# Keeping the second attention's turned h for the shared expert, and one barrier instead of two between phases

## The chip, the cores and the metric

One core of a Trainium2 chip runs the whole program. The metric is device microseconds for one launch. The text uses these names for the engines: TensorE (PE in the rows, PEld for its weight loads), VectorE (DVE), ScalarE (ACT), GpSimd (POOL) and SyncE (SP), which issues most DMAs.

## The reference

Two layers, each of a cross-attention and a mixture of experts, on x of 16 batches x 128 tokens x 256 values:

```python
x = x + attention0(layernorm(x), ctx, ctx, bias, mask)          # 16 heads of 16
x = x + moe0(layernorm(x))                                       # top 2 of 14 experts, hidden 512
x = x + attention1(layernorm(x), ctx, ctx, causal or padding)    # 16 heads of 16
h = layernorm(x)
x = x + shared(h) + routed(h)    # shared expert, hidden 1024, and top 2 of 8 experts, hidden 1024
```

where `shared(h) = gelu(h @ Wfc_s + bfc_s) @ Wproj_s + bproj_s`, and the router's logits are `h @ Wr`. All in fp32.

## The kernel before

A tile is the 128 tokens of one batch (B = 16 tiles). The program is a row of six phases, written one after the other in `build`: `attention0`, `route_and_project` (routing of layer 0 and keys and values of the second attention), `experts` of layer 0 (45 slots of 128 rows), `attention1`, `shared_expert` (with the routing of layer 1), `experts` of layer 1 (39 slots). Each phase opens a block, in which every engine has its own hand-written list of instructions; semaphores alone order them across engines. What stands in the list is the order, nothing schedules it anew.

A block ends in a barrier of all engines. After it `end_phase` (L66 to L70) has GpSimd clear the semaphores of the phase (L68) and then sets a second barrier (L70), so that no engine begins the next phase before they are zero. I number the boundaries 1 to 5 by the phase that they end; a sixth ends the program.

`attention1` goes through the tiles in a loop in which a tile's stages are spread over several turns. For tile b, GpSimd's `layer_norm` (L1016) writes the normalized rows h into `Hn[:, b]`, SyncE's `store_h` (L960) writes them to memory for the later gather, five turns after the tile's own, TensorE's `turn_h` (L1155) transposes them into PSUM, ScalarE's `h_out` (L1309) copies that into the one buffer `hT`, and `logits` (L1194) multiplies `hT` by the router's weights. Tile 0 of the shared expert is done at the end of this phase, between the last attention tiles: `turn_shared` (L1161) transposes h of tile 0 a second time, VectorE copies it to `hx` (L1425), and `up_shared` (L1174) and `down_shared` (L1183) do the two products. Before that, `combine` (L1349) reads `Hn[:, b]` of layer 0.

`shared_expert` does the tiles 1 to 15 (N = 15). TensorE's list for turn n is: `up(n + 1)`, 16 fp32 matmuls in the program (the trace records each as 2); `turn(n + 2)`, the 2 transposes of h of a later tile (L1917); `down(n)`, 8 matmuls of 256 columns; and in turns 2 to 9 some products that invert the routing. ScalarE copies each turned tile from PSUM to `xT` (L1960) and applies the gelu (L1967). Only four PSUM banks take the results of `up`, so TensorE can do four of the eight hidden pieces before the first gelu. VectorE begins the phase with the top two of the logits; their difference (`diff`, L1610) goes through an exponential on ScalarE (L1973), which needs another table than the gelu, so that the gelu's table is loaded (L1974) after it. SyncE loads 16 MB of expert weights meanwhile, and stores the sums.

## Time and profile before

| | us |
|---|---|
| time before, median of 3 runs | 975.86 |
| lowest and highest of them | 975.44 and 976.85 |
| the profiled execution | 974.42 |
| its span, first to last instruction | 972.5 |
| TensorE busy | 922.1 (95% of the span) |
| VectorE, ScalarE, GpSimd busy | 511.5, 501.7, 436.8 |
| mean granted TensorE clock | 0.982 of 2.4 GHz |

The phases begin in the trace at about 0, 184.2, 221.8, 398.3, 554.2 and 676.2 us. The chain of work that ended last is, followed back, TensorE's from 678.7 us to 961.3 us, all of the last phase. A group of rows below gives one view of the trace. In a timeline a row has its start in us, its length, the engine, the line of the code, the operation with output and inputs, the count of merged instructions, and in square brackets the idle time before it and who ended it. A row of one line of the code has durations in ns (lowest, median, highest) and the starts of its first and last instruction in us.

### The profile page before, as it was taken

The numbers are of one execution on the slowest core, as the hardware profiler recorded it, in microseconds if no ns is written. First come the engines' busy times: TensorE is split into PE (matmuls) and PEld (weight loads), VectorE is DVE, ScalarE is ACT, GpSimd is POOL, SyncE is SP. The second block draws the span as 40 slices with busy tenths as digits, with TensorE's granted clock in tenths as the row PEclk, the third lists the DMA queues.
The fourth block names the chain that finished last, engine by engine and source line by source line (L and its number), as shares of the span: only waits on it lengthen the run. The fifth ranks groups of instructions, "written<-read, shape, count | busy, mean of one in ns | idle before, by whom it ended". The sixth has DMA issues, their size and how long they took to land. (4 is left out here: it accounts for less than half of the span.)

```text
span 972.5 us, 25476 instructions
## 1 busy us (share of the span) xinstructions
PE 922.1 (95%) x7420; PEld 830.1 (85%) x7421; DVE 511.5 (53%) x2152; ACT 501.7 (52%) x1425; POOL 436.8 (45%) x570
## 2 busy tenths in 40 slices
PE   5999999798999999789999899998999999999996
PEld 4788888697999999668878799997999999999996
DVE  3988988563444344279999553321333333333331
ACT  3877778233434343289999553332434334334332
POOL 5778885103555554535664420001244434434433
PEclk9999999899999999889999999999999999999999
DMA  8776674742222222353321299001111111111110
GB/s 263 236 229 202 185 240 149 286 137 93 70 70 70 71 69 65 127 168 88 91 62 44 69 376 341 18 28 33 34 59 53 51 56 46 47 53 54 50 33 1
DMA packets 98569, 107.36 MB, mean 110 GB/s; under 512 B 9858, under 2 KB 83992, under 8 KB 98234
## 3 DMA queue, kind: packets, MB, share of 16 engines
q1 hardware_dynamic: 88160, 80.76, 25.7%
q0 software_dynamic: 9936, 25.32, 8.7%
q8 instruction: 40, 0.66, 0.3%
q10 hardware_dynamic: 394, 0.31, 0.1%
q14 instruction: 39, 0.32, 0.1%
HBM read 86.68 MB, written 21.50 MB: 111 GB/s over the span
## 5 line engine op out<-in xcount | busy, mean ns | idle before, releaser
L2104 PEld LDWEIGHTS experts_bank<-xT,wp 128*128 128x128 f32 x1968 | 235.6, 194 | 8.4 <-issue 4.3
L2104 PE MATMUL experts_bank<-xT,wp 128*128 128x128 f32 x1968 | 236.3, 277 | 3.8 <-issue 2.0
L2146 ACT ACTIVATE Hn<-experts_bank,vecT 128x128 f32<-128x128 f32 x312 | 114.5, 367 | 167.5 <-PE experts_bank L2104 146.3
L1737 POOL DMA_INDIRECT rows<-token_rows,src x84 | 82.6, 984 | 179.9 <-DVE dst L1732 108.1
L2114 PE MATMUL experts_bank<-w,Hn 128*128 x624 | 142.6, 382 | 0.0
L2163 DVE COPY wp<-w 128x1024 f32 x123 | 90.4, 735 | 96.4 <-PE experts_bank L2104 95.5
L2114 PEld LDWEIGHTS experts_bank<-w,Hn 128*128 128x128 f32 x624 | 115.5, 190 | 15.8
L2146 ACT ACTIVATE hid<-experts_bank,vecT 128x128 f32<-128x128 f32 x180 | 66.0, 367 | 101.5 <-PE experts_bank L2104 92.0
L2114 PE MATMUL experts_bank<-w,hid 128*128 x360 | 85.0, 379 | 0.0
L2057 POOL DMA_INDIRECT out_dram<-yb,dst x39 | 41.2, 1056 | 90.2 <-DVE yb L2186 90.2
L1286 ACT ACTIVATE E<-U,mn 128x128 f32<-128x128 f32 x256 | 79.6, 392 | 2.2 <-DVE mn L1368 2.2
L648 ACT ACTIVATE w<-w,mn 128x128 f32<-128x128 f32 x256 | 80.0, 400 | 0.9 <-DVE mn L765 0.9
L2054 POOL DMA_INDIRECT token_outputs<-yb,dst x45 | 51.1, 1136 | 61.9 <-DVE yb L2177 61.9
L346 POOL TENSOR_TENSOR w<-w 128x1024 f32<-128x1024 f32 x32 | 75.6, 2365 | 0.9 <-DVE w L712 0.9
L1967 ACT ACTIVATE hid<-shared_bank,vecT 128x128 f32<-128x128 f32 x120 | 43.7, 367 | 60.5 <-PE shared_bank L1926 53.2
L2183 DVE TENSOR_TENSOR yb<-experts_bank,b 128x256 f32<-128x256 f32 x39 | 16.6, 425 | 110.5 <-PE experts_bank L2114 110.5
L2065 POOL DMA_INDIRECT X<-out_dram,dst x39 | 42.1, 1079 | 65.7 <-DMA out_dram<-yb,dst 62.6
L2114 PEld LDWEIGHTS experts_bank<-w,hid 128*128 128x128 f32 x360 | 65.0, 190 | 7.0
L1368 DVE CUSTOM_DVE_ANT_0 U<-attn_bank,M 128x128 f32<-128x128 f32 x256 | 57.8, 287 | 9.5 <-PE attn_bank L1101 9.3
L1926 PE MATMUL shared_bank<-xT,w_shared 128*128 128x128 f32 x480 | 57.9, 280 | 1.2 <-ACT hid L1967 1.2
L765 DVE CUSTOM_DVE_ANT_0 w<-attn_bank,w 128x128 f32<-128x128 f32 x256 | 57.4, 285 | 2.9 <-PE attn_bank L489 1.9
L1926 PEld LDWEIGHTS shared_bank<-xT,w_shared 128*128 128x128 f32 x480 | 56.5, 196 | 1.8 <-ACT hid L1967 1.5
(286 smaller groups left out, 1569.6 us busy)
## 6 DMA issues: line engine op xcount, KB each, us to landing
w<-in_fside_Bx16xSxS_dram SPq DMA_DIRECT2D x32, 512.0 KB, 4.9
w<-in_L_ffn_w_dram SPq DMA_DIRECT2D x28, 512.0 KB, 6.4
w<-in_L_ffn_Wfc_dram SPq DMA_DIRECT2D x8, 1024.0 KB, 13.8
w<-in_L_ffn_Wproj_dram SPq DMA_DIRECT2D x8, 1024.0 KB, 12.7
token_rows<-Hn SPq DMA_DIRECT2D x32, 128.0 KB, 4.6
y<-token_outputs SPq DMA_DIRECT2D x16, 256.0 KB, 3.2
ctx<-in_ctx_dram SPq DMA_DIRECT2D x26, 128.0 KB, 4.5
keys_values<-WT SPq DMA_DIRECT2D x12, 256.0 KB, 2.0
```

The costliest lines, as they stand in the source:

```text
L346: pool.tensor_tensor(fs[b % 2][:, heads], fs[b % 2][:, heads], bcast(amb[:, b:b + 1], [P, 8, P]), ALU.add).then_inc(bias_ready[half], 1)
L648: last = act.activation(E_[:, h], U[:, h], ACT.Exp, bias=mn[b % 2][:, h:h + 1], scale=-1.0)
L765: last = dve.tensor_tensor_reduce(U[:, h], scores_of(h), fs[b % 2][:, h], -twice, BIG, ALU.add, ALU.min, mn[b % 2][:, h:h + 1])
L1286: last = act.activation(E_[:, h], U[:, h], ACT.Exp, bias=mn[b % 2][:, h:h + 1], scale=-1.0)
L1368: last = dve.tensor_tensor_reduce(U[:, h], scores_of(h), c["M1"][:], -1.0, BIG, ALU.add, ALU.min, mn[b % 2][:, h:h + 1])
L1737: pool.indirect_dma_start(out=weights["rows"][:, n % 2], out_offset=None, in_=c["hn"], in_offset=bass.IndirectOffsetOnAxis(ap=routing["src ...
L1926: last = pe.matmul(HB[f % 4][:, 0:P], w1[:, i, f * P:(f + 1) * P], xT[n % 2][:, i], start=(i == 0), stop=(i == DC - 1))
L2054: pool.indirect_dma_start(out=c["yg"], out_offset=at_rows, in_=yb[n % 2][:], in_offset=None).then_inc(y_stored[n % 2], 16)
L2104: last = pe.matmul(HB[f % 4][:, 0:P], piece[:, i, (f % CF) * P:(f % CF + 1) * P], xT[par][:, i], start=(i == 0), stop=(i == DC - 1))
L2114: last = pe.matmul(Y[par][:, 0:D], hid[par][:, f], weights["w2"][:, bass.ds(e * (FC * D) + f * D, D)], start=(f == 0), stop=(f == FC - 1))
L2146: act.activation(hid[par][:, f], HB[f % 4][:, 0:P], moe.act, bias=bias).then_inc(hid_ready, 1)
L2163: dve.tensor_copy(wp[par if NP == 1 else q][:], of[:, :, q * PIECE:(q + 1) * PIECE]).then_inc(wp_ready, 1)
```

## The change

There are two parts.

**The barriers.** `end_phase` now only notes the semaphores of the phase as retired. The barrier at the end of each block stays; the second one is gone at boundaries 1 to 5. GpSimd clears the retired semaphores within the next phase: after its seven iotas in the two routing phases (L1842 and L1898 of the new file), after its four memsets in `attention1` (L1041), and after two gathers in `experts` (L2042). Semaphores of a phase and of the next are so never the same ones. At the program's end, clear and barrier stand as before.

**The turned h.** In `attention1` the normalized rows go into a ring of three buffers `hrow`, from which they are stored and transposed, and `h_out` copies the transposed tile from PSUM into `Hn[:, b]`, where it stays. The router's logits, tile 0 of the shared expert and `shared_expert` read it there. `turn_shared` with its copy, and all of `turn` and `in_out` of `shared_expert` go. `layer_norm` from tile 3 on waits until the tile three before has been transposed and its store has landed; the stores of layer 1 count on three semaphores, one for each buffer.

```diff
         def end_phase():
-            nc.clear_and_free_semaphores(phase_sems)
+            c["retired"] = list(phase_sems)
             phase_sems.clear()
-            nc.all_engine_barrier()
...
         experts(nc, sem, alloc, c, moe1, routing, weights, out)
-        end_phase()
+        nc.clear_and_free_semaphores(phase_sems)
+        nc.all_engine_barrier()
...
 def attention1
-        hT = sb("hT", [P, DC, P])
+        hrow = [sb(f"hrow{i}", [P, D]) for i in range(3)]
...
-        hx, hid = y[0][:, 0].rearrange("p (c t) -> p c t", c=DC), U[:, 0:FC]
+        hx, hid = c["Hn"][:, 0].rearrange("p (c t) -> p c t", c=DC), U[:, 0:FC]
...
             def store_h(b):
                 sp.wait_ge(h_ready, b + 1)
-                sp.dma_start(token_rows(c["hn"], b), c["Hn"][:, b]).then_inc(c["hn_stored"][1], 16)
+                sp.dma_start(token_rows(c["hn"], b), hrow[b % 3][:]).then_inc(c["hn_stored"][1][b % 3], 16)
...
-                pool.tensor_scalar(c["Hn"][:, b], c["X"][:, b], rs[:], nm[:], ALU.mult, ALU.add).then_inc(h_ready, 1)
+                if b >= 3:
+                    pool.wait_ge(hT_done, b - 2)
+                    pool.wait_ge(c["hn_stored"][1][b % 3], 16 * (b // 3))
+                pool.tensor_scalar(hrow[b % 3][:], c["X"][:, b], rs[:], nm[:], ALU.mult, ALU.add).then_inc(h_ready, 1)
...
+            nc.clear_and_free_semaphores(c["retired"])
             for b in range(-3, B + 1):
...
-            def turn_shared():
-                pe.wait_ge(h_ready, 1)
-                for i in range(DC):
-                    last = pe.transpose(IN[:, D + i * P:D + (i + 1) * P], c["Hn"][:, 0, i * P:(i + 1) * P], c["ident"][:])
-                last.then_inc(hx_done, 1)
...
             def h_out(b):
                 act.wait_ge(hT_done, b + 1)
-                if b >= 1:
-                    act.wait_ge(lg_done, b)
-                act.activation(hT[:].rearrange("p c t -> p (c t)"), IN[:, 0:D], ACT.Copy).then_inc(hT_ready, 1)
+                act.activation(c["Hn"][:, b], IN[:, 0:D], ACT.Copy).then_inc(hT_ready, 1)
...
-                if b == B - 1:
-                    dve.wait_ge(hx_done, 1)
-                    dve.tensor_copy(hx.rearrange("p c t -> p (c t)"), IN[:, D:2 * D]).then_inc(hx_ready, 1)
...
 def shared_expert
             route_counters(pool, r, iotas_ready)
+            nc.clear_and_free_semaphores(c["retired"])
...
             def up(n):
-                pe.wait_ge(xT_ready, n + 1)
...
-                        last = pe.matmul(HB[f % 4][:, 0:P], w1[:, i, f * P:(f + 1) * P], xT[n % 2][:, i],
+                        last = pe.matmul(HB[f % 4][:, 0:P], w1[:, i, f * P:(f + 1) * P], c["Hn"][:, S0 + n, i * P:(i + 1) * P],
...
-            turn(0)
-            turn(1)
             pe.wait_ge(shared["loaded"], 16 * 3)
             up(0)
...
-                if n + 2 < N:
-                    turn(n + 2)
                 down(n)
...
-            in_out(0)
-            in_out(1)
             act.wait_ge(diff_ready, 1)
...
                 tile(n)
-                if n + 1 < N:
-                    in_out(n + 1)
...
 def experts
             for n in range(2, AHEAD):
                 gather(n)
+            nc.clear_and_free_semaphores(c["retired"])
```

How the instructions stand now, at the two places on which the sum rests. A semaphore's name in brackets can be that of an earlier phase, whose number it got. First GpSimd at boundary 1, from the end of `attention0` to the first gather, before:

```order
L357 TENSOR_SCALAR Hn<-X,rs,nm 128x256 [waits nm_ready_117]
L145 UNCONDITIONAL_BRANCH
L68 ISA [waits barrier_Pool_Activation_PE_DVE_SP_gather]
L1846 UNCONDITIONAL_BRANCH [waits barrier_Pool_Activation_PE_DVE_SP_gather]
L1564 IOTA iota_e 128x14
...
L1572 IOTA pad_row 128x45
L1737 DMA rows<-token_rows,src 128x256 [waits hn_stored0,xn_ready_72]
```

and after:

```order
L358 TENSOR_SCALAR Hn<-X,rs,nm 128x256 [waits nm_ready_117]
L146 UNCONDITIONAL_BRANCH
L1839 UNCONDITIONAL_BRANCH [waits barrier_Pool_Activation_PE_DVE_SP_gather]
L1555 IOTA iota_e 128x14
...
L1563 IOTA pad_row 128x45
L1842 ISA
L1728 DMA rows<-token_rows,src 128x256 [waits hn_stored0_0,made_197]
```

The clear (the ISA row) has moved from between two barriers to behind the iotas, and one of the two waits for a barrier is gone. Second TensorE at the start of `shared_expert`, before:

```order
L1917 MATMUL shared_bank<-ident,Hn 128x128 x4
L1926 MATMUL shared_bank<-xT_348,w_shared 128x128 x16
L1926 MATMUL shared_bank<-xT_349,w_shared 128x128 x16
L1581 MATMUL shared_bank<-both,before 128x128
...
L1917 MATMUL shared_bank<-ident,Hn 128x128 x2
L1935 MATMUL shared_bank<-w_shared,hid_350 128x256 x8
L1926 MATMUL shared_bank<-xT_348,w_shared 128x128 x16
L1917 MATMUL shared_bank<-ident,Hn 128x128 x2
```

and after:

```order
L1911 MATMUL shared_bank<-Hn,w_shared 128x128 x32
L1572 MATMUL shared_bank<-both,before 128x128
L1573 MATMUL shared_bank<-both,ones 128x128
L1920 MATMUL shared_bank<-w_shared,hid_348 128x256 x8
L1911 MATMUL shared_bank<-Hn,w_shared 128x128 x16
```

The transposes (L1917) are gone, four at the start and two in front of each of the next thirteen `down`s, and nothing has come in their place.

## Rows read from the trace of the kernel before

**Rows 1.** Part 1 of the page: busy us, share of the span, instructions.

```profile
PE 922.1 (95%) x7420; PEld 830.1 (85%) x7421; DVE 511.5 (53%) x2152; ACT 501.7 (52%) x1425; POOL 436.8 (45%) x570
```

**Rows 2.** Busy time by stage, TensorE clock, DMA share, GB/s; columns are named first.

```profile
core 0: us, PE busy (x) PEld busy (x) DVE busy (x) ACT busy (x) POOL busy (x), PEclk, DMA share, GB/s
...
398.30:552.50 154.20, 147.05 (x1546) 119.80 (x1546) 124.47 (x705) 129.49 (x387) 77.09 (x180) 0.96 0.30 92
560.00:674.40 114.40, 114.31 (x798) 107.77 (x798) 35.93 (x158) 47.05 (x133) 8.37 (x12) 1.00 0.46 163
676.20:961.40 285.20, 283.30 (x1936) 265.71 (x1937) 105.12 (x191) 114.68 (x313) 116.36 (x112) 0.99 0.16 47
```

**Rows 3.** TensorE's queue at boundaries 1, 2, 4: first barrier, second barrier, and the clear.

```profile
L145 PEldq EVENT_SEMAPHORE  x2: 51/51/51, 182.2 to 183.1; - x2
...
L70 PEldq EVENT_SEMAPHORE  x1: 51/51/51, 184.1 to 184.1; - x1
...
L68 POOLq EVENT_SEMAPHORE_RANGE_CLEAR  x1: 527/527/527, 183.4 to 183.4; - x1
...
L1751 PEldq EVENT_SEMAPHORE  x2: 51/51/51, 219.9 to 221.2; - x2
...
L70 PEldq EVENT_SEMAPHORE  x1: 51/51/51, 221.7 to 221.7; - x1
...
L879 PEldq EVENT_SEMAPHORE  x2: 51/51/51, 552.6 to 553.3; - x2
...
L70 PEldq EVENT_SEMAPHORE  x1: 51/51/51, 554.2 to 554.2; - x1
```

**Rows 4.** Timeline at the start of the shared expert: start, us, engine, line, work [idle].

```profile
555.42 3.42 PE L1926 MATMUL shared_bank<-xT,w_shared 128*128 128x128 f32 x16
...
557.79 0.19 DVE L1610 TENSOR_TENSOR diff<-top 128x16 f32<-128x16 f32 x1
...
558.25 1.28 ACT L1974 ACT_TABLE_LOAD   x1
...
559.65 6.43 ACT L1967 ACTIVATE hid<-shared_bank,vecT 128x128 f32<-128x128 f32 x16
...
560.06 5.62 PE L1926 MATMUL shared_bank<-xT,w_shared 128*128 128x128 f32 x48 [1.21 <-ACT hid L1967]
```

**Rows 5.** Timeline of TensorE alone inside the shared expert, one turn and the last one.

```profile
569.64 3.73 PE L1926 MATMUL shared_bank<-xT,w_shared 128*128 128x128 f32 x32
573.21 0.38 PE L1917 MATMUL shared_bank<-ident,Hn 128*128 128x128 f32 x2
573.43 3.62 PE L1935 MATMUL shared_bank<-w_shared,hid 128*128 128x256 f32 x16
...
660.05 0.38 PE L1917 MATMUL shared_bank<-ident,Hn 128*128 128x128 f32 x2
```

**Rows 6.** Stretches around boundary 4, columns as in Rows 2.

```profile
552.20:555.60 3.40, 1.19 (x8) 0.66 (x7) 1.72 (x19) 0.38 (x1) 1.36 (x8) 1.00 0.11 8
555.60:559.05 3.45, 3.24 (x16) 2.95 (x15) 3.38 (x34) 2.68 (x4) 3.45 (x6) 0.51 0.89 337
```

**Rows 7.** Timeline where the second attention runs out of tiles.

```profile
537.11 0.42 DVE L1425 COPY y<-attn_bank 128x256 f32<-128x256 f32 x1
...
537.58 1.16 PE L1174 MATMUL attn_bank<-y,w_shared 128*128 128x128 f32 x8 [0.20 <-DVE y L1425]
```

**Rows 8.** Ring of h: store of h(0), making of h(3), landing times of the stores.

```profile
444.45 0.47 SPq L960 DMA_DIRECT2D token_rows<-Hn  x1
...
458.23 0.56 POOL L1016 TENSOR_SCALAR Hn<-X,rs,nm 128x256 f32<-128x256 f32 x1
...
DMA to landing us min/median/max: 1.7/2.7/4.3
```

More of the change, by code:

```diff
@@ L99, in build @@
         c["late_loaded"] = nc.alloc_semaphore("late_loaded")
-        c["hn_stored"] = [nc.alloc_semaphore(f"hn_stored{layer}") for layer in range(2)]
+        c["hn_stored"] = [[nc.alloc_semaphore(f"hn_stored{layer}_{i}") for i in range(n)] for layer, n in ((0, 1), (1, 3))]
         moe0 = Moe(0, 14, 512, a["L0_ffn_w1"], a["L0_ffn_w2"], a["L0_ffn_b2"], ACT.Gelu)
@@ L258, in store_h @@
                 sp.wait_ge(h_ready, b + 1)
-                sp.dma_start(token_rows(c["hn"], b), c["Hn"][:, b]).then_inc(c["hn_stored"][0], 16)
+                sp.dma_start(token_rows(c["hn"], b), c["Hn"][:, b]).then_inc(c["hn_stored"][0][0], 16)
             load_fs(0, 0)
@@ L929, in attention1 @@
         s_done = sem("s_done")
-        hx_done, hx_ready, up_done, hid_ready, down_done = (
-            sem("hx_done"), sem("hx_ready"), sem("up_done"), sem("hid_ready"), sem("down_done"))
+        up_done, hid_ready, down_done = sem("up_done"), sem("hid_ready"), sem("down_done")
         late_turned, late_T_ready = sem("late_turned"), sem("late_T_ready")
@@ L1154, in turn_h @@
                 for i in range(DC):
-                    last = pe.transpose(IN[:, i * P:(i + 1) * P], c["Hn"][:, b, i * P:(i + 1) * P], c["ident"][:])
+                    last = pe.transpose(IN[:, i * P:(i + 1) * P], hrow[b % 3][:, i * P:(i + 1) * P], c["ident"][:])
                 last.then_inc(hT_done, 1)
-            def turn_shared():
-                pe.wait_ge(h_ready, 1)
-                for i in range(DC):
-                    last = pe.transpose(IN[:, D + i * P:D + (i + 1) * P], c["Hn"][:, 0, i * P:(i + 1) * P], c["ident"][:])
-                last.then_inc(hx_done, 1)
             def up_shared(first, end):
                 if first == 0:
-                    pe.wait_ge(hx_ready, 1)
+                    pe.wait_ge(hT_ready, 1)
                     pe.wait_ge(shared["loaded"], 16 * 3)
@@ L1193, in logits @@
                 for i in range(DC):
-                    last = pe.matmul(Y[:, 0:E], hT[:, i], wr[:, i], start=(i == 0), stop=(i == DC - 1))
+                    last = pe.matmul(Y[:, 0:E], c["Hn"][:, b, i * P:(i + 1) * P], wr[:, i], start=(i == 0), stop=(i == DC - 1))
                 last.then_inc(lg_done, 1)
@@ L1244, in _ @@
                     turn_e(b, 1)
-                if b == B - 1:
-                    turn_shared()
                 if has(b - 1):
@@ L1422, in _ @@
                     minima(b, 3)
-                if b == B - 1:
-                    dve.wait_ge(hx_done, 1)
-                    dve.tensor_copy(hx.rearrange("p c t -> p (c t)"), IN[:, D:2 * D]).then_inc(hx_ready, 1)
                 if has(b + 3):
@@ L1743, in gather_first @@
     pool.wait_ge(made, 4)
-    pool.wait_ge(c["hn_stored"][moe.layer], 16 * B)
+    stored = c["hn_stored"][moe.layer]
+    for i, sem in enumerate(stored):
+        pool.wait_ge(sem, 16 * ((B + len(stored) - 1 - i) // len(stored)))
     for n in range(2):
@@ L1868, in shared_expert @@
         two = range(2)
-        xT = [sb(f"xT{i}", [P, DC, P]) for i in two]
         hid = [sb(f"hid{i}", [P, FC, P]) for i in two]
@@ L1877, in shared_expert @@
                         for k in (r["hot"][0], r["hot"][1], r["tmp"], r["over"])]
-        bank = [stack.enter_context(nc.psum_tensor(f"shared_bank{i}", [P, 512], F32)) for i in range(8)]
-        T, R, HB, Y = bank[0], bank[1], bank[2:6], bank[6:8]
+        bank = [stack.enter_context(nc.psum_tensor(f"shared_bank{i}", [P, 512], F32)) for i in range(7)]
+        R, HB, Y = bank[0], bank[1:5], bank[5:7]
         slots_of = R[:, 2 * B * moe.E:2 * B * moe.E + 2 * S]
@@ L1884, in shared_expert @@
         bias_added = sem("bias_added")
-        xT_done, xT_ready = sem("xT_done"), sem("xT_ready")
         hid_done, hid_ready = sem("hid_done"), sem("hid_ready")
@@ L1912, in _ @@
         def _(pe):
-            def turn(n):
-                if n >= 1:
-                    pe.wait_ge(xT_ready, n)
-                for i in range(DC):
-                    last = pe.transpose(T[:, i * P:(i + 1) * P], c["Hn"][:, S0 + n, i * P:(i + 1) * P], c["ident"][:])
-                last.then_inc(xT_done, 1)
             def up(n):
-                pe.wait_ge(xT_ready, n + 1)
                 for f in range(FC):
@@ L2070, in _ @@
                 gather(n)
+            nc.clear_and_free_semaphores(c["retired"])
             if out is not None:
```

5 lines of the change are left out of this document (removed).

## The prediction

> **What bounds the kernel now.** I read the page's busy times first: TensorE is busy for 95% of the span, no other engine for more than 53% [rows 1]. An average over phases says little, so the second view is the busy time by stage [rows 2]. From 560.0 to 674.4 us, the shared expert, TensorE is busy for 114.31 of 114.40 us, while ScalarE has 47 us of work and VectorE 36. From 676.2 to 961.4 us it is 283.3 of 285.2. In the second attention TensorE has 147 of 154 us, with ScalarE at 129 and VectorE at 124: nearly bound, with less room beside it. So anything taken from TensorE's list in the shared expert should be seen whole, work taken from ScalarE or VectorE there should not be seen, and time in which all engines stand still is on the path whatever bounds the phases. That is what the third view looks for: TensorE's own semaphore instructions at the boundaries [rows 3].
>
> **The second barrier.** At boundary 1 TensorE leaves the first barrier at 183.1 us and the second at 184.1 us, and between them stands GpSimd's clear of 0.53 us: 1.0 us. At boundary 2 it is 221.2 to 221.7, 0.5 us; at boundary 4 it is 553.3 to 554.2, 0.9 us [rows 3]. Boundaries 3 and 5 read like 2, 0.5 us each, so there are three of that kind. The sum is 1.0 + 3 x 0.5 + 0.9 = 3.4 us. No engine does anything in these stretches, and each next phase starts with a chain that begins at its barrier, so I count them whole. The bounds are 0, if what follows waits for something older than the barrier, and 3.4.
>
> The clears do not vanish. They stand in GpSimd's list behind the iotas, the memsets or two gathers. What is queued behind them is the bias additions of the shared expert, the clipping of the first tile in the attention, and the third gather and first fetch of sums in the experts. A clear with its drain is at most about 0.7 us by the one at boundary 1 (0.53 us, [rows 3]). GpSimd has 8.4 us of work in 114 us of the shared expert and half of the time free in the attention [rows 2], so I count nothing; if the first tile's chain of the attention had no room, it would be 0.7 us once.
>
> **The transposes of the shared expert.** TensorE starts the transposes of a turn at 573.21 us and the next product at 573.43 us: 0.22 us from start to start, though a transpose is drawn as longer, since they overlap. There are thirteen such pairs, the last at 660.05 [rows 5], all in the stretch in which TensorE is full. 13 x 0.22 = 2.9 us, bounds 2.7 and 3.0 for the rounding of the starts. The fifteen copies of ScalarE there lie beside TensorE's work and give nothing.
>
> The first two transposes of the phase are another matter. They stand ahead of the first sixteen recorded matmuls, which run from 555.42 to 558.84, but then TensorE waits 1.21 us for ScalarE's gelu [rows 4]. The gelu starts at 559.65, directly behind the load of its table (558.25, 1.28 us), that waits for the exponential, and that for VectorE's difference at 557.79 [rows 4]. VectorE begins at the barrier and its list does not change. So the early start of TensorE only makes the wait longer: gain 0 for the transposes, beyond the 0.9 us already counted. VectorE's list is the next late thing, and it was before.
>
> **The second transpose of tile 0.** At the end of the attention two transposes and a copy go. VectorE's copy runs from 537.11 to 537.53 us and TensorE's product starts at 537.58, after 0.20 us of idle time [rows 7]. Without them TensorE could start 0.22 + 0.20 = 0.4 us earlier. ScalarE's exponentials of tile 15 do not come earlier by that, so TensorE meets them again soon after. I take 0.2 us, bounds 0 and 0.4.
>
> **The ring.** GpSimd makes h(3) at 458.23 us; in the changed kernel that waits for the store of h(0), which SyncE issues at 444.45 us. The stores land within 4.3 us at the longest, so it is there by 448.8, 9.4 us early [rows 8]. Every tile has the same distance, since store and h both move on by one tile per turn. The transposition of the tile three before stands in TensorE's list ahead of the product that h needs. Cost 0. ScalarE loses a wait for the logits that had long been met, VectorE reads the same buffer as before: 0.
>
> **The clock.** Here the change can lose something. In the stretch from 552.2 to 555.6 us TensorE is busy for 1.19 of 3.40 us, and in the one behind it, to 559.05 us, the granted clock is 0.51, that is the 1.2 GHz level [rows 6]. The sixteen matmuls that fell into it took 3.42 us [rows 4]; at 2.4 GHz thirty-two take 3.57 us from start to start [rows 5], so sixteen take 1.8. These 1.6 us cost nothing before, since TensorE waited for the gelu anyway. In the changed kernel the sixteen matmuls start right behind the barrier at full clock, are through about 1.9 us later, and then TensorE stands still until the gelu. The gelu's first result lets it go on at 560.06, 5.9 us after the barrier's 554.2, so the pause grows from 1.2 to about 4 us. A slow stretch after that pause falls on matmuls that bound the phase. The bounds are 0 and 1.6 us; I take 1.1, since part of the slow stretch may still lie in the pause.
>
> The Trainium skill (TensorE: Matmul & The Clock Gate, Part 1) says that throttled is the default state and that activity releases it, and Part 4 that transposes do not count as activity. The rows agree with the first: the clock fell behind a thin stretch. By the page a pause of 4 us costs the clock nearly always, which would put the term at its upper bound.
>
> **Sum.** 3.4 + 2.9 + 0.2 - 1.1 = 5.4 us. Against the profiled execution that is 974.42 - 5.4 = 969.0. That execution lies 1.4 us below the median of the three runs, 975.86, and the change will be measured against a median: 975.86 - 5.4 = 970.5 us.
>
> **The rivals.**
>
> (a) *The slow clock costs more.* Besides the pause at boundary 4, a second slow stretch may move from hidden onto bound work, at another boundary, for the phases now meet the clock's ups and downs at other moments. For it speaks that boundary 4's slow stretch was wholly hidden; against it that each other pause gets shorter. Price: 1.6 instead of 1.1 and 1.6 more, 975.86 - 6.5 + 3.2 = 972.6. [...]
>
> (b) *The barriers give nothing.* If a phase's start were held by something else, such as the fetch of its code or a DMA issued long before, only the transposes pay: 975.86 - 2.9 - 0.2 + 1.1 = 973.9. Against it: TensorE starts each phase within about 0.1 us of the second barrier's release, at 184.2 behind 184.1.
>
> (c) *The clock comes back.* With shorter pauses one boundary no longer loses the clock, and the pause at boundary 4 costs nothing: 975.86 - 6.5 - 1.6 = 967.8. Against it: the pauses shrink only by 0.5 to 1.0 us.
>
> (d) *Slower: the ring holds the attention.* GpSimd would stand in `layer_norm`, and `v_in` and `normed` of the next tiles are queued behind it, for which TensorE waits. It decides from the point at which a store lands more than 458.23 - 444.45 = 13.8 us after its issue. Thirteen tiles wait so; at 1 us each the time is 975.86 - 5.4 + 13 = 983.5. Against it stand 4.3 us as the longest landing [rows 8].
>
> **How the numbers follow.** A run of this kernel can be told from no change at about 0.2%, 2.0 us. Chances: forecast 0.68, own range 968.8 to 972.0 (terms at their bounds: 3.4 + 3.0 + 0.4 = 6.8 at best, 3.4 + 2.7 + 0 - 1.6 = 4.5 at worst, and some tenths for the scatter of 1.4 us of the runs); (a) 0.07; (b) 0.12, half of it within 0.2%; (c) 0.08; (d) 0.05. Faster: 0.68 + 0.07 + 0.06 + 0.08 = 0.89; same 0.06; slower 0.05. The range of 8 in 10 takes in the forecast and (a), and the near side of (b) and (c): 968.0 to 973.2.
>
> **What would show it.** In the changed profile: no second stop behind a block's barrier, and first work of the next phase 0.1 us after it; the product of `down` directly behind that of `up` in the shared expert, 0.22 us earlier in each turn; TensorE idle for some 4 us at the start of the shared expert with the gelu still 5.4 us behind the barrier; a clock below 1.00 right behind that pause; the tiles of the attention at an unchanged distance, and no idle time of GpSimd in front of `hrow`. A longer distance of the tiles, or a phase whose first row is later than its barrier by half a microsecond, would prove me wrong.

## The result: faster by 9 us, more than forecast, and the profile after

| us | before | changed |
|---|---|---|
| median | 976.36 of 4 runs (975.44 to 976.91) | 967.16 of 4 runs (967.05 to 967.47) |
| the profiled execution | 974.42 | 967.47 |
| its span | 972.5 | 965.3 |
| TensorE busy | 922.1 | 917.9 |
| mean granted TensorE clock | 0.982 | 0.983 |

The ratio is 0.9905, 95% interval 0.9886 to 0.9923: 9.2 us less, where 5.4 were forecast, and 967.2 lies below the range of 968.0 to 973.2. Between the two profiled executions the gain is 6.95 us. The kernel before scatters more than the first three runs showed: 77 runs of it, taken beside the experiments, lie between 972.8 and 979.8 us, 28 of them above 977, with a median of 976.0. Ten runs of the changed kernel lie between 965.7 and 968.0. So the profiled execution of the kernel before, 974.4, is one of its shorter ones, and 2.3 of the 9.2 us can't be found by comparing these two profiles.

Part 1 of the changed kernel's page, which answers to [rows 1]:

```profile
PE 917.9 (95%) x7388; PEld 826.6 (86%) x7389; DVE 511.5 (53%) x2151; ACT 496.9 (51%) x1410; POOL 436.7 (45%) x570
```

TensorE has 32 recorded instructions and 4.2 us less, ScalarE 15 and 4.8 us less. TensorE's queue at the boundaries 1, 2 and 4 in the changed kernel (instruction, count, ns, start of first and last), and GpSimd's clear behind boundary 1, answer to [rows 3]:

```profile
L146 PEldq EVENT_SEMAPHORE  x2: 51/51/51, 182.4 to 183.3; - x2
...
L1744 PEldq EVENT_SEMAPHORE  x2: 51/51/51, 220.1 to 221.4; - x2
...
L880 PEldq EVENT_SEMAPHORE  x2: 51/51/51, 549.6 to 550.2; - x2
...
L1842 POOLq EVENT_SEMAPHORE_RANGE_CLEAR  x1: 526/526/526, 184.6 to 184.6; - x1
```

There is one stop where there were two, and the phases begin 0.1 us behind it: 183.4, 221.5, 550.3. The clear of boundary 1 lies 1.3 us into the next phase.

What the stops cost is best read as TensorE's idle time in front of the first matmul of phases 2 to 6. It was 2.12, 2.02, 4.53, 1.73 and 1.86 us and is 1.10, 1.50, 3.71, 0.84 and 1.34 us, 3.8 us less in all. At boundary 3 it is 0.8 us less, where the forecast has 0.5. The second release stood 0.54 us behind the first there, as forecast; the other 0.3 us are GpSimd's part of the first barrier, which took 0.38 us before and takes 0.1 us now. The rows of boundary 3, before and changed:

```profile
398.33 0.82 PE L1054 MATMUL attn_bank<-ident,WT 128*128 128x128 f32 x4 [4.53 <-PEq L70]
```

```profile
395.50 0.63 PE L1058 MATMUL attn_bank<-ident,WT 128*128 128x128 f32 x4 [3.71 <-PEq L1980]
```

The start of the shared expert in the changed kernel, all engines, as a timeline; it answers to [rows 4]:

```profile
550.33 1.19 DVE L1596 MAX8 top<-LG 128x8 f32<-128x8 f32 x16 [0.38 <-PEq L880]
550.33 2.02 PE L1911 MATMUL shared_bank<-Hn,w_shared 128*128 128x128 f32 x16 [0.84 <-PEq L880]
...
553.85 0.40 DVE L1601 TENSOR_TENSOR diff<-top 128x16 f32<-128x16 f32 x1
...
554.51 1.28 ACT L1947 ACT_TABLE_LOAD   x1
...
555.92 1.60 ACT L1942 ACTIVATE hid<-shared_bank,vecT 128x128 f32<-128x128 f32 x5
556.32 6.28 PEld L1911 LDWEIGHTS shared_bank<-Hn,w_shared 128*128 128x128 f32 x41 [4.16 <-ACT hid L1942]
556.32 6.36 PE L1911 MATMUL shared_bank<-Hn,w_shared 128*128 128x128 f32 x40 [3.97 <-ACT hid L1942]
```

The first sixteen matmuls now take 2.02 us instead of 3.42, then TensorE stands still for 3.97 us until the gelu at 555.92, which is 5.7 us behind the barrier (5.4 before). The stretches of that start, with busy time of each engine, granted clock (the column after POOL), DMA share and GB/s, answer to [rows 6]:

```profile
550.30:552.40 2.10, 2.02 (x16) 1.86 (x16) 2.04 (x29) 1.27 (x1) 1.21 (x8) 1.00 0.40 78
552.40:556.30 3.90, 0.00 (x0) 0.00 (x0) 3.83 (x25) 1.99 (x5) 3.90 (x7) 1.00 1.03 382
556.80:560.20 3.40, 3.40 (x19) 3.40 (x18) 1.63 (x6) 1.71 (x5) 3.40 (x6) 0.50 1.05 389
```

Behind the pause the clock is at its lower level of 1.2 GHz for 3.4 us, and TensorE is busy in all of it: 19 matmuls there, where a full-clock stretch of this length has 32 (below). Before, the slow stretch lay ahead of a wait.

TensorE alone inside the shared expert, as in [rows 5], and the ring as in [rows 8] (making of h, stores, landings), changed kernel:

```profile
563.86 3.62 PE L1920 MATMUL shared_bank<-w_shared,hid 128*128 128x256 f32 x16
567.31 3.73 PE L1911 MATMUL shared_bank<-Hn,w_shared 128*128 128x128 f32 x32
570.88 1.46 PE L1920 MATMUL shared_bank<-w_shared,hid 128*128 128x256 f32 x6
...
L1019 POOL TENSOR_SCALAR hrow<-X,rs,nm x16: 554/555/556, 432.6 to 546.2; 128x256 f32<-128x256 f32 x16
...
L960 SPq DMA_DIRECT2D token_rows<-hrow x16: 319/432/466, 442.0 to 546.8; - x16
...
DMA to landing us min/median/max: 1.7/2.8/4.2
```

The product of `down` stands directly behind that of `up`: from 567.31 to 570.88 are 3.57 us, and in [rows 5] it was 3.57 + 0.22. The tiles of the attention are (546.2 - 432.6) / 15 = 7.57 us apart. In the kernel before they were 7.62 us apart. The difference stands in three places. Between the tiles 13 and 14, where the second transpose of tile 0 is gone, the distance is 7.22 instead of 7.50 us, and so in every kernel with the turned h. Between the tiles 7 and 8 and between 10 and 11 it is 7.8 instead of 7.9 and 8.05 us, 0.4 us in all, and so in every kernel with one barrier per boundary, `barriers_only` among them, and in no other; why is open.

To see where the 7.2 us of the two spans went, I cut both at the first matmul of each phase. The time of a boundary counts to the phase that it ends. All times are us.

| phase with its boundary | before | changed | gain | forecast |
|---|---|---|---|---|
| 1 `attention0` | 184.2 | 183.4 | 0.9 | 1.0 |
| 2 `route_and_project` | 37.6 | 38.1 | -0.5 | 0.5 |
| 3 `experts`, layer 0 | 176.5 | 174.0 | 2.4 | 0.5 |
| 4 `attention1` | 155.9 | 154.8 | 1.1 | 1.1 |
| 5 `shared_expert` | 122.0 | 120.4 | 1.5 | 2.3 |
| 6 `experts`, layer 1, to the end | 296.3 | 294.5 | 1.8 | 0 |

Phases 2 and 3 differ from the forecast mostly by the clock. At the start of phase 3 the stretch of the kernel before and the same one of the changed kernel read (columns as above):

```profile
224.00:228.80 4.80, 4.35 (x24) 4.38 (x25) 1.55 (x3) 1.47 (x4) 1.18 (x1) 0.64 0.35 99
...
223.90:228.00 4.10, 3.94 (x35) 3.97 (x36) 1.40 (x3) 2.46 (x7) 0.89 (x1) 1.00 0.36 107
```

In exchange the slow stretch around boundary 1 is longer in the changed kernel, 10.2 us instead of 6.8. Further profiles of both kernels show that this comes and goes from execution to execution (below). Phase 6 is another matter. The end of the kernel before and of the changed one, as timelines:

```profile
964.93 0.43 DVE L2183 TENSOR_TENSOR yb<-experts_bank,b 128x256 f32<-128x256 f32 x1 [2.51 <-PE experts_bank L2114]
966.53 1.02 POOL L2065 DMA_INDIRECT X<-out_dram,dst  x1 [2.80 <-issue]
968.76 0.48 DVE L2186 SCALAR_TENSOR_TENSOR yb<-yb,share,X 128x256 f32<-128x256 f32 x1 [3.41 <-DMA X<-out_dram,dst]
```

```profile
959.11 0.42 DVE L2155 TENSOR_TENSOR yb<-experts_bank,b 128x256 f32<-128x256 f32 x1 [2.51 <-PE experts_bank L2086]
959.27 1.02 POOL L2036 DMA_INDIRECT X<-out_dram,dst  x1 [1.35 <-DMA out_dram<-yb,dst]
961.50 0.49 DVE L2158 SCALAR_TENSOR_TENSOR yb<-yb,share,X 128x256 f32<-128x256 f32 x1 [1.97 <-DMA X<-out_dram,dst]
```

The last fetch of sums starts 1.60 us behind VectorE's bias addition before, and 0.16 us after. Before, nothing recorded ends GpSimd's idle time ahead of it ("issue"). That is 1.44 us which no step of the prediction has, and it repeats: the time from the end of TensorE's last drain to the end of the span is 7.72 or 7.73 us in all six profiles of the kernels whose only clears stand between the barriers, and 6.3 to 6.7 us in all nine with clears inside the phases (6.27 or 6.28 in the six of the changed kernel and its variants, 6.58 in `spare_clear`).

### The profile page after: what moved, and what is told of

It reads as the page before. It is cut to its first block and busy times, and to the rows that moved or that the text cites. A ratio compares the mean times of both kernels' runs of the same rounds, so it can differ in the third digit from the quotient of the medians.

```text
span 965.3 us, 25316 instructions
## 1 busy us (share of the span) xinstructions
PE 917.9 (95%) x7388; PEld 826.6 (86%) x7389; DVE 511.5 (53%) x2151; ACT 496.9 (51%) x1410; POOL 436.7 (45%) x570
## 5 line engine op out<-in xcount | busy, mean ns | idle before, releaser
L1911 PE MATMUL shared_bank<-Hn,w_shared 128*128 128x128 f32 x480 | 58.2, 281 | 4.8 <-ACT hid L1942 4.0
L1911 PEld LDWEIGHTS shared_bank<-Hn,w_shared 128*128 128x128 f32 x480 | 56.8, 197 | 5.6 <-ACT hid L1942 4.2
```

Of the source, the lines that this page charges most:

```text
L1911: last = pe.matmul(HB[f % 4][:, 0:P], w1[:, i, f * P:(f + 1) * P], c["Hn"][:, S0 + n, i * P:(i + 1) * P], start=(i == 0), stop=(i == DC - 1))
```

## The experiments

Each ratio is against the runs of the kernel before on the same chip. Because of the scatter the time of the profiled execution stands beside the median.

**The two parts apart, and both kernels again.** `barriers_only` takes all edits of `end_phase` and the clears, and nothing of the turned h; `turned_only` the rest. `base_again` and `after_again` are the two kernels.

```diff
 barriers_only
         def end_phase():
-            nc.clear_and_free_semaphores(phase_sems)
+            c["retired"] = list(phase_sems)
             phase_sems.clear()
-            nc.all_engine_barrier()
...
 turned_only
         def end_phase():
             nc.clear_and_free_semaphores(phase_sems)
             phase_sems.clear()
             nc.all_engine_barrier()
...
-            turn(0)
-            turn(1)
             pe.wait_ge(shared["loaded"], 16 * 3)
```

> The kernel before, unchanged, timed again beside itself. Theory A (the profiled execution of before, 974.42 us, was a lucky one; the clock and the last fetch of sums scatter by some us from execution to execution): times between 974.4 and 977, median about 976.3, and in this profile more of TensorE's matmuls at 1.2 GHz, or the fetch of the last sums again more than 1 us after the landing that it waits for. Theory B (nothing scatters, the first profile shows what every execution does): the profile again at 974.4 and the same slow stretches.

> Only the barriers are changed, h is turned twice as before. Theory A (a second barrier costs the distance between the two releases, 3.4 us in all, and up to one slow stretch of the clock of 1.6 us comes or goes): 971 to 973 us against 976.4. Theory B (a barrier costs more than that distance, since the phase behind it starts warmer or its DMAs earlier): 969 to 970.5, 6 us or more off.

> Only the turned h is kept, both barriers stand as before. Theory A (13 pairs of transposes at 0.22 us and 0.2 us at the end of the attention, less a slow stretch of 1.6 us behind the longer pause at the start of the shared expert): 1.5 to 3.1 us off, 973.3 to 974.9 against 976.4. Theory B (the stores or copies of the attention matter too): more than 4 us off, and a shorter distance of the attention's tiles than 7.78 us.

> The changed kernel, unchanged, timed again. 967.2 us as before by both theories. Theory A: the slow stretches of the clock lie at other moments in this profile than in the first, in number between five and seven, and their place decides within 1 us. Theory B: they lie at the same places.

| kernel | median us (range, runs) | ratio, 95% | profiled execution | phases 1 to 6 of it |
|---|---|---|---|---|
| before, beside these | 975.74 (973.05 to 979.79, 23) | | | |
| `base_again` | 978.08 (973.7 to 979.72, 12) | 1.0023 (1.0009 to 1.0038) | 973.7 | 183.5, 37.4, 176.4, 155.9, 122.0, 296.6 |
| `barriers_only` | 969.2 (968.25 to 973.81, 6) | 0.9949 (0.9929 to 0.9968) | 968.83 | 182.3, 37.7, 175.7, 153.5, 123.2, 294.8 |
| `turned_only` | 973.06 (971.18 to 977.56, 12) | 0.9985 (0.9967 to 1.0003) | 971.9 | 183.2, 37.6, 176.7, 155.0, 120.6, 297.1 |
| `after_again` | 967.04 (965.65 to 967.95, 6) | 0.9914 (0.9899 to 0.9928) | 967.12 | 182.6, 37.4, 175.7, 153.0, 120.4, 296.0 |

The turned h gives 2.7 us by the medians and 974.42 - 971.9 = 2.5 by the profiles; the forecast for its terms with the clock's was 2.9 + 0.2 - 1.1 = 2.0. The barriers give 6.5 and 5.6 (4.9 against the profiled execution of `base_again`); the forecast was 3.4. So the step that failed is the barriers'.

Two things hide in these 5.6 us. Phase 5 of `barriers_only` is 1.2 us longer than before, although its boundary is 0.5 us shorter: TensorE's pause for the gelu grows there from 1.21 to 2.88 us, and the slow stretch of the clock, 555.0 to 558.4 us there, lies on the matmuls that begin behind it at 555.15. So the clock's loss at boundary 4 comes with either part alone, and the two parts do not simply add. Phase 4, in exchange, is 2.4 us shorter, of which the boundary gives 0.9; slow stretches cover 7.3 us of TensorE's work there instead of 11.6. That `base_again`, the same instructions, has a median 2.3 us above the other runs of the kernel before shows how little a median of it means within some 2 us. Phases 2, 3, 4 and 6 differ by up to 1.8 us between the profiles of the changed kernel and `after_again`, with slow stretches of the clock at other places.

**What clears inside the phases do, without any barrier gone.** `clears_moved` keeps both barriers and clears within the next phase. `spare_clear` is the kernel before with both barriers and its clears, and at the four places of the changed kernel one more clear, of a semaphore that nobody uses.

```diff
 clears_moved
         def end_phase():
-            nc.clear_and_free_semaphores(phase_sems)
+            c["retired"] = list(phase_sems)
             phase_sems.clear()
             nc.all_engine_barrier()
...
 spare_clear, def experts
             for n in range(2, AHEAD):
                 gather(n)
+            nc.clear_and_free_semaphores([nc.alloc_semaphore(f"spare_{moe.layer}")])
```

> The kernel before with the clears moved into the next phase and both barriers kept. It parts the barrier's price from the clear's. By the releases in the trace of before a boundary with a short clear took 0.5 us and the clears are 0.53, 0.13, 0.09, 0.43 and 0.13 us: with the clears gone from between the barriers some 1.5 us are saved, 974.5 against 976, and barriers_only is 1.9 us below it. If the upper heap of before comes from the clears between barriers, it is missing here; if from the barriers, it stays.

> The kernel before, both barriers and its clears between them kept, and in each later phase one more clear of a semaphore that nobody uses, at the places where the changed kernel has its clears. Three questions. First, the tail: in every kernel whose clears stand inside the phases the last fetch of sums starts 0.26 to 0.30 us after TensorE has drained, in every other 1.70 us, and the span ends 1.4 us earlier. If that goes with the place of GpSimd's instructions in its stream, the tail is 6.3 us here as well and the time is 1.4 us shorter; if with the missing clears or barriers, it stays 7.7. Second, the drain of 7.15 us at boundary 3 in the kernel with the clears moved: if a clear ahead of the second barrier is what keeps that drain short (0.04 us in the kernel before), it is short here and the time lies between 973 and 978; if the clears inside the phases make it long, the time is about 983. Third, what a clear within a phase costs: by the sum of the prediction nothing, at most 0.7 us for each, 2.8 us in all.

`spare_clear`: 973.43 us (971.88 to 978.75, 10 runs) against 975.73 (972.82 to 979.1, 13), ratio 0.9983 (0.9962 to 1.0004), its profiled execution 978.75. The tail of its profile:

```profile
970.55 0.42 DVE L2187 TENSOR_TENSOR yb<-experts_bank,b 128x256 f32<-128x256 f32 x1 [2.51 <-PE experts_bank L2118]
970.71 1.03 POOL L2068 DMA_INDIRECT X<-out_dram,dst  x1 [1.36 <-DMA out_dram<-yb,dst]
```

The fetch follows the addition at once, as in the changed kernel. The three shortest runs are 971.9, 972.0 and 972.2, those of the kernel before beside it 972.8, 973.4 and 973.8; the interval of the ratio takes in 1, so the times alone do not show the gain, and the profile does: the tail is 6.58 us instead of 7.72. The early fetch thus comes with clears that stand inside the phases, and not with a barrier or a clear that is gone. It isn't the length of GpSimd's list: the trace has 694 GpSimd instructions in `barriers_only`, where the fetch is early, 705 in the kernel before and 719 in `turned_only`, where it is late. Why GpSimd issues it late the trace doesn't say. A fetch of its code is not seen: from 960 to 971 us of the kernel before, the only packets are those of the indirect transfers.

```profile
## 3 DMA queue, kind: packets, MB, share of 16 engines
q0 software_dynamic: 96, 0.00, 0.6%
```

The clears themselves are not on the path here: phases 2 to 5 of `spare_clear` take 38.1, 176.1, 156.5 and 122.2 us, within 0.4 us of some profile of the kernel before. Yet each costs GpSimd more than the 0.7 us of the prediction, since a drain goes ahead of it that takes 0.9 to 2.6 us.

`clears_moved`: 983.16 us (979.57 to 983.63, 6 runs) against 976.13 (974.26 to 979.55, 11), ratio 1.006 (1.0038 to 1.0082), so 7 us slower than the kernel before, and not the 1.5 us faster that was expected. The profile shows where. GpSimd's queue instructions of the second barrier in its profile, and the first work behind boundary 3:

```profile
L70 POOLq DRAIN  x5: 46/211/7150, 182.3 to 683.7; - x5
...
405.10 1.28 ACT L1262 ACT_TABLE_LOAD   x1 [14.27 <-PEq L70]
405.11 0.53 POOL L1036 MEMSET kside<- 128x512 f32 x1 [9.50 <-POOLq L70]
```

One drain of GpSimd takes 7.15 us, the one between the two barriers of boundary 3, and all engines wait for it; the phase in front of it is 184.0 us long instead of 176.5. At the other four boundaries this drain takes 0.05 to 0.23 us. In the kernel before the drains of the second barrier take 0.04 us in each of its profiles, behind a first drain that belongs to the clear and takes 0.08 to 0.19 us. So a second barrier without a clear was cheap at four boundaries and cost 7 us at one. What the long drain waits for is open: in its first 2.9 us the trace has two packets of the queues that load instructions, in its last 4.3 us no DMA packet at all.

**The clock behind the pause at boundary 4.** `after_busy4` is the changed kernel with fifteen matmuls of the identity by itself, into a bank that nobody reads, in the pause of 3.97 us.

```diff
+def keep(pe, to, c, n):
+    for i in range(n):
+        pe.matmul(to[:, 0:P], c["ident"][:], c["ident"][:], start=True, stop=True)
...
             def up(n):
                 for f in range(FC):
+                    if n == 0 and f == 4:
+                        keep(pe, bank[7], c, 15)
                     if FC * n + f >= 4:
```

> The changed kernel with fifteen matmuls of the identity with itself, into a free PSUM bank, in TensorE's pause at the start of the shared expert (results not used; the computation is complete). Clock theory (the pause drops the clock and the slow stretch behind it costs 1.6 us): no slow stretch there, the phase shorter by 1.2 to 1.6 us, 965.5 us. Rival (the phase is longer than the sum for another reason, such as VectorE's chain): the stretch is gone, the time stays at 967.0.

965.0 us (964.37 to 969.4, 7 runs) against 976.13, ratio 0.9879 (0.986 to 0.9898). The stretches of pause and of the 3.4 us from 0.5 us behind its end, columns as above:

```profile
557.30:561.30 4.00, 3.38 (x31) 3.19 (x29) 3.93 (x26) 2.00 (x5) 4.00 (x7) 1.00 1.03 392
561.80:565.20 3.40, 3.40 (x32) 3.40 (x32) 1.63 (x6) 2.81 (x9) 3.40 (x6) 1.00 1.04 386
```

The clock stays at 1.00, and 32 matmuls stand where 19 stood. The phase takes 118.8 us instead of 120.4: the pause cost 1.6 us, the upper bound that the prediction gave. The median is 2.2 us below the changed kernel's first one, and 2.0 below that of `after_again`. Not all of that need be this pause: in this profile boundary 5 has no slow stretch either, and phase 6 takes 293.1 us instead of 294.5 and 296.0.

**All pauses.** `after_busy` puts such matmuls into the pauses of TensorE at all boundaries and where the second attention starts; `before_busy` does it to the kernel before.

```diff
                 if b == B + 2:
+                    keep(pe, TE, c, 1)
...
             turn(1)
+            keep(pe, bank[5], c, 4)
...
             turn(1, 1, 0)
+            keep(pe, Y[1], c, 7)
...
             paired(pe, n_slots, slot)
+            if out is None:
+                keep(pe, T[0], c, 13)
```

> The changed kernel with such matmuls in the pauses of TensorE at all five boundaries and in the ramp of the second attention. Clock theory: at most one or two slow stretches left after the first 180 us, 4 to 6 us off the changed kernel, 961 to 963 us, and the executions closer together. Rival (the clock's slow stretches lie under other waits anyway): within 1.6 us of the changed kernel.

> The kernel before with the same matmuls in its pauses. It asks for the scatter of before (973.0 to 979.8 us, in two heaps near 974.3 and 978.8). Clock theory: the scatter is that of slow stretches, so it shrinks to 2 us or less and the upper heap goes: 968 to 971 us. Rival (the upper heap is of another cause, tied to the second barriers and the clears): two heaps stay, some 4.5 us apart, only both earlier.

`after_busy`: 957.5 us (955.82 to 960.14, 5 runs), ratio 0.9807 (0.9783 to 0.9831), phases 183.8, 35.6, 174.0, 150.1, 118.8, 293.0. That is 9.7 us less than the changed kernel, where 4 to 6 were expected. `before_busy`: 967.88 (966.42 to 971.08, 6 runs), ratio 0.9916 (0.9893 to 0.9938), phases 184.4, 35.8, 174.8, 151.7, 123.3, 295.3. The two differ by 10.4 us in the medians and 9.75 in the profiled executions. The cores' row of each:

```profile
core 0: 955.3 us, clock 0.998
```

```profile
core 0: 965.4 us, clock 0.996
```

By phase the difference is 0.6, 0.2, 0.8, 1.6, 4.5 and 2.3 us. It is nearly the change without the clock, but not in phase 5, which is 1.4 us longer in `before_busy` than in the kernel before itself. Its start shows why:

```profile
547.85 3.38 PE L1945 MATMUL shared_bank<-xT,w_shared 128*128 128x128 f32 x16
551.02 3.09 PE L1459 MATMUL shared_bank<-ident 128*128 128x128 f32 x24
553.95 2.29 PE L1945 MATMUL shared_bank<-xT,w_shared 128*128 128x128 f32 x19
```

The first sixteen matmuls are still slow, 3.38 us at a granted clock of 0.53; the pause ahead of them is not filled. The added ones (L1459) come only behind them and hold TensorE until 553.95, 7.26 us behind the phase's first instruction. In the kernel before it went on after 5.80 us. So the added matmuls cost 1.5 us there, and without them the two would differ by about 8.6 us in span. The rows read so far give 3.8 for the stops, 0.4 for the two distances in the attention, 0.3 for the transpose of tile 0, 2.9 for those of the shared expert and 1.4 for the tail, 8.8 in all. Phase by phase it fits less well: phase 6 has 0.9 us more than the tail, phases 1 and 2 together 0.7 us less than their stops.

**The ring.** `stores_later` is the changed kernel with the stores of h issued one turn later.

```diff
-                if has(b - 5):
-                    store_h(b - 5)
+                if has(b - 6):
+                    store_h(b - 6)
...
-            for b in range(B - 5, B):
+            for b in range(B - 6, B):
                 store_h(b)
```

> The changed kernel with the stores of h in the second attention issued one turn later (six turns behind the tile, not five). A turn takes 6.9 us, so a store that was issued 13.8 us before its buffer is written again is now issued about 6.9 us before. My theory: the stores land within 4.3 us, GpSimd still waits for nothing, and the time is the changed kernel's 967.1 within 0.2%. Rival (d) of the prediction, that the ring holds the attention: the slack of 13.8 us is less than it seems, since the store stands in the queue behind nine other transfers of its turn; then GpSimd has idle time ahead of hrow, and the time grows by up to 13 x 1 us or more, 970 to 980.

968.72 us (966.55 to 969.11, 4 runs) against 975.73, ratio 0.9923 (0.9904 to 0.9943), by 0.2% not to be told from the changed kernel's 0.9905 and 0.9914. The rows of the making of h in its profile, and the stores with their landings:

```profile
L1019 POOL TENSOR_SCALAR hrow<-X,rs,nm x16: 554/555/557, 432.8 to 546.4; 128x256 f32<-128x256 f32 x16
...
L960 SPq DMA_DIRECT2D token_rows<-hrow x16: 319/446/1778, 450.1 to 547.0; - x16
...
DMA to landing us min/median/max: 1.7/2.5/3.9
```

The first store is issued 8.1 us later, the tiles keep their distance of 7.57 us, phase 4 takes 153.0 us as in `after_again`, and GpSimd's waits name only VectorE. Even with a turn less of slack the ring holds nobody, so rival (d) falls. Two turns less were not tried: the program would then wait for itself.

**Where the long executions have their 5 us.** `before_look` is the kernel before once more, `before_start` has eight of the idle matmuls at its very start, where TensorE waits for loads, and `after_busy_start` is `after_busy` with the same eight.

```diff
             pe.wait_ge(ident_ready, 1)
+            keep(pe, Y, c, 3)
             turn_w(0)
+            keep(pe, Y, c, 4)
             turn_w(1)
...
             for b in range(-1, B + 3):
+                if b == 0:
+                    keep(pe, O, c, 1)
```

> The kernel before once more, for its profile. Its times scatter between about 973 and 980 us and gather around 974.2 and 979, while ten runs of the changed kernel lie between 965.7 and 968.0. Question: where do the 5 us of a long execution stand? Theory L (loads): in the first phase, whose first 24 us wait for loads from memory; then a long execution has its second phase beginning at about 188 us instead of 184.2, as the one long profile of the changed kernel with work in the pause at boundary 4 had (188.5), and all boundaries have the same lengths. Theory B (boundaries): a drain of GpSimd at a boundary is sometimes long, as the one of 7.15 us in the kernel with the clears moved and both barriers kept; then one boundary is longer by about 5 us and the first phase has its 184.2 us. A time of 974 would say nothing; one of 976 or more tells them apart.

> The kernel before with eight more matmuls of TensorE (the identity by itself, into a bank nobody reads) at its very start, where TensorE waits for loads: three ahead of the first turned weight, four between the first and the second, one ahead of the first scores. Both long executions in the records (969.4 and 978.75 us) have TensorE at half its speed until about 27 us (the first scores take 2.09 us), all eleven ordinary ones only until about 15 us (1.15 us), and their second phase begins at 188.5 and 189.0 instead of 182.3 to 184.4. If it is TensorE's start that makes the 5 us, the early work ends it: no execution above about 975, the lowest at 971 to 974, and a median of 972 to 974 against the kernel before's 976, that is 2 to 3 us. The rival: late loads make both, the slow TensorE and the 5 us; then executions near 978 stay, about half of them, and the median stays at 975 to 976.

> The changed kernel with work in all of TensorE's pauses at the boundaries (957.5 us) and the same eight matmuls at the start besides. By the theory of the start: the clock is up some us earlier, 1 to 2 us less, 955.5 to 957.0, and no execution at 960. By the rival: 957.5 as before, with an execution at 960 now and then.

`before_look` came out at 974.77 us, one of the shorter executions, with phases 183.3, 38.1, 176.5, 156.3, 122.0 and 296.7, and so does not answer the question. But the profiled executions of `spare_clear` (978.75) and of `after_busy4` (969.4) are the longest of their kernels, by 5.3 and 4.4 us over the median, and both have a first phase of 189.0 and 188.5 us, where the thirteen other profiles have 182.3 to 184.4. TensorE at the start, first in the kernel before, then in `spare_clear`:

```profile
17.07 1.15 PE L489 MATMUL attn_bank<-kside,qT 32*128 32x256 f32 x16 [1.06 <-DVE kside L742]
18.15 0.66 PE L411 MATMUL attn_bank<-ident,w 128*128 128x128 f32 x4
...
21.81 1.16 PE L449 MATMUL attn_bank<-xcT,WT 128*128 128x128 f32 x8 [0.69 <-ACT xcT L630]
```

```profile
17.14 2.09 PE L489 MATMUL attn_bank<-kside,qT 32*128 32x256 f32 x16 [1.06 <-DVE kside L742]
19.16 1.11 PE L411 MATMUL attn_bank<-ident,w 128*128 128x128 f32 x4
...
24.64 2.07 PE L449 MATMUL attn_bank<-xcT,WT 128*128 128x128 f32 x8 [0.69 <-ACT xcT L630]
```

The same matmuls start at nearly the same moment and take 2.09 us instead of 1.15. A transpose of 128 columns takes 0.42 us until about 29 us in these two profiles and 0.27 us from there on; in the other thirteen it gets fast at 13 to 17 us. 0.42 us is also what it takes in the stretches at 1.2 GHz. The column of the granted clock shows 1.00 in both executions, but it is no reading there: the trace's first record of the clock is at 28.8 us in `spare_clear` and 29.3 in `after_busy4`, at 13.0 to 16.5 us in the others, and ahead of it the view puts 1.00. That TensorE's slow start makes the whole 5 us is likely, not shown: nothing here changed it. My cure failed. `before_start` has 975.87 us (973.62 to 980.46, 12 runs) against 975.72 (973.17 to 978.18, 17), ratio 1.0008 (0.9993 to 1.0023), with three runs above 978. Its profile, an ordinary one, has TensorE slow until about 14 us in spite of the added matmuls, seven of which stand in the first 6.5 us and the eighth at 14.3. So they do not set when TensorE gets fast. `after_busy_start` has 957.28 us (956.26 to 958.44, 4 runs), ratio 0.9812 (0.9789 to 0.9835): the same as `after_busy`.

## Why the prediction was wrong

**The second barriers, 3.4 us.** One stop is gone at each boundary, as forecast, each next phase starts 0.1 us behind its one barrier, and phases 1 and 4 gain 0.9 and 1.1 us. But the two parts apart gave 5.6 us by the profile and 6.5 by the median for the barriers, not 3.4. This is the step that failed, in three of its terms. The clears in GpSimd's list were put at nothing, with bounds of 0 and 0.7 us of loss, and no row excluded a gain; in fact the tail of phase 6 got 1.4 us shorter with them, and 1.1 us in `spare_clear`, which has both barriers. The stops were put at 3.4 us and measured 3.8 by TensorE's idle time, since boundary 3 was read from the second barrier alone; GpSimd's part of the first barrier is as short in `spare_clear` (0.08 us), so its 0.3 us, too, do not need a barrier gone. And two tile distances of the attention, which the prediction had as unchanged, gave 0.4 us. The tail has its experiment, the other two only their rows; why the fetch comes early, and why the two distances shrink, stays open.

**The reference point.** I took the gain off 975.86 us, the median, although the sum was made against an execution of 974.42. The two are not the same thing here. All three profiles of the kernel before are of executions of 973.7 to 974.8, while 28 of its 77 runs are above 977; of the changed kernel no run of ten is 1 us above its median. The measured gain over the medians is 9.2 us, over the profiles 6.95. The 2.3 us between them are the 1.9 us by which the first profiled execution lies below its kernel's median and the 0.3 us by which the second lies above. Long executions are rarer without the second barriers: more than 4 us above the shortest run of their own kernel are 3 of 36 runs there, 29 of 77 of the kernel before, and 13 of 46 of the other kernels with both barriers. For two long executions the place is shown, the first phase, which the barriers do not touch. Why one barrier less should make them rarer is open, and with four to twelve runs of each kernel I don't claim that it does.

**The transposes, 2.9 us.** Right: `down` starts 3.57 us behind `up` instead of 3.79 (3.62 instead of 3.83 in the turns that invert the routing), in all thirteen turns; with the clock held up the phase is 118.8 us, 3.2 less than before, for a forecast of 2.9 and 0.5 for boundary 5. Most of what is missing is the gelu, which lets TensorE go on 5.99 us behind the phase's first matmul instead of 5.80.

**The clock, 1.1 us.** Right in mechanism and place: a pause of 3.97 us (forecast about 4), gelu 5.7 us behind the barrier, granted clock 0.50 behind the pause, on matmuls that bound the phase. The size was 1.6 us by `after_busy4`, its upper bound. The Trainium skill (TensorE: Matmul & The Clock Gate, Part 1), by which throttled is the default and activity releases it, would have set the term there, and the trace agrees.

**The second transpose of tile 0, 0.2 us**, and **the ring, 0**: both right. The distance of the tiles 13 and 14 is 0.28 us shorter in each kernel with the turned h. The ring holds nobody, with one turn less of slack either.

**The rivals.** (a) happened in part, 0.5 us more at boundary 4; the second slow stretch did not come. (b) falls with `barriers_only`. (c) gives 967.8 and is nearest in number, by luck: the pause at boundary 4 cost its 1.6 us, and no boundary kept its clock by the change. At the start of phase 3 the clock stayed up in the changed kernel's first profile, and in `after_again` it did not. (d) falls with `stores_later`.

What adds up, in the profiled executions: 3.8 stops + 0.4 distances + 2.9 transposes + 0.3 transpose of tile 0 + 1.4 tail - 1.6 clock - 0.2 later gelu = 7.0 us, against 6.95 measured. That sum is made after the fact, and a slow stretch of the clock more or less (1.6 us) would move the measured number away from it.

## What to carry to other kernels

Two barriers with a clear between them cost all engines what GpSimd needs for it, here 0.5 to 1.0 us a boundary, and in this kernel the clear could lie inside the next phase at no cost that shows, if the semaphores are other ones. Take the barrier away with it: a second barrier without the clear cost 7 us at one of five boundaries. Fill TensorE's pauses at phase boundaries with matmuls that nobody reads: by the medians it took 9.7 us off the changed kernel and 8.3 us off the one before, about as much as the change itself. Fill only up to the moment at which the real work can go on: twelve matmuls too late cost 1.5 us. Before forecasting a median, ask for the scatter of the kernel, and take the gain off the profiled execution.

## What was not expected of the hardware

- Clears on GpSimd far ahead change when a later instruction of it is issued: the last indirect fetch started 1.6 us behind its neighbour on VectorE in the six profiles without clears inside the phases, and 0.15 to 0.20 us behind it in the nine with them, with the same instructions around it.
- A drain of GpSimd took 7.15 us in one kernel, 3.1 us behind its last indirect DMA; at the same place the kernel before has two drains, of 0.14 and 0.04 us.
- TensorE's speed at the start of the program rises at 13 to 17 us in thirteen executions and at about 29 in two, whose first phase is 4 to 5 us longer. The trace has no record of the clock ahead of that point, and a granted clock of 1.00 shown there is no reading.
- Fifteen matmuls of 128 columns in a pause of 4 us kept the granted clock at 1.00; the pause alone was followed by 3.4 us at 0.50.
